# Products for the next chunk's maxima at other steps of the two spare PSUM banks

## The reference

```
q, k, v   = Wq x + bq, Wk x + bk, Wv x + bv          # layer 0: 32, 32, 256 channels
attn      = softmax(q^T k, over the query index i)    # scores[b, i, j], axis=1
x1        = gamma * (v attn) + x

theta     = conv1x1(x1)                               # layer 1: 32 channels, 4096 positions
phi, g    = maxpool2(conv1x1(x1))                     # 32 and 128 channels, 1024 positions
attention = softmax(theta^T phi, over j)
y         = gamma * conv1x1(g attention) + x1
```

## Time and profile before

| | |
|---|---|
| median of 3 runs | 2719.68 us (2712.09 to 2726.18) |
| profiled execution | 2717.54 us, of which the span is 2715.7 us |
| mean granted TensorE clock | 0.986 |
| PE busy | 2610.4 us, 96% |
| DVE busy | 2036.5 us, 75% |
| ACT busy | 1741.6 us, 64% |
| POOL busy | 1979.4 us, 73% |
| products for maxima, 128x512 into aux (L954) | 1097 |
| reductions of these (L740) | 1097, 683 ns each |

### The profile page before, as it was taken

How to read it: one execution, slowest core, us unless ns; L and a number is a source line. 1 busy time by engine, 2 the same in 40 slices (tenths; PEclk the granted TensorE clock), 3 DMA queues, 4 the chain that set the end, 5 groups by cost and what they waited for, 6 DMA issues and landing times.

```text
span 2715.7 us, 38345 instructions
## 1 busy us (share of the span) xinstructions
PE 2610.4 (96%) x11632; PEld 2078.7 (77%) x11632; DVE 2036.5 (75%) x3351; ACT 1741.6 (64%) x3171; POOL 1979.4 (73%) x1546
## 2 busy tenths in 40 slices
PE   7999999989999999998999999999899999999988
PEld 6788788777678888887678888888667888888765
DVE  7678777767777777776777777787677777877665
ACT  5566666667756666666775666666676666666566
POOL 3677777767867777775886777777588777777668
PEclk9999999999999999999999999999899999999989
DMA  2000000012110000001220000000121000000011
GB/s 90 1 16 16 17 24 17 24 40 71 63 32 21 20 23 18 17 16 41 70 78 24 17 24 16 17 16 17 47 79 63 16 16 16 17 17 16 17 47 63
DMA packets 45552, 85.28 MB, mean 31 GB/s; under 512 B 5032, under 2 KB 5160, under 8 KB 45352
## 3 DMA queue, kind: packets, MB, share of 16 engines
q1 hardware_dynamic: 37720, 68.41, 7.6%
q10 hardware_dynamic: 7632, 14.42, 1.8%
HBM read 49.03 MB, written 33.55 MB: 30 GB/s over the span
## 4 chain that ended last, share of the span: by engine, by line
PE 78%; DVE 12%; issue 5%; ACT 2%; POOL 1%; DMA 1%; SPq 0%; ACTq 0%; POOLq 0%; DVEq 0%
PE o_ps L914 16%; PE o_ps L917 16%; PE o_ps L918 16%; PE s_ps L891 9%; PE aux L954 8%; DVE mx L740 5%; DVE acc L702 3%; PE aux L928 2%; PE aux L992 1%; PE aux L975 1%; PE aux L932 1%; DVE aux L781 1%; PE aux L971 1%; POOL prob_l L502 1%; ACT queries L589 1%
## 5 line engine op out<-in xcount | busy, mean ns | idle before, releaser
L502 POOL TENSOR_TENSOR prob_l<-prob,prob_h 128x512 fp32r<-128x512 f32 x1280 | 1665.7, 1309 | 628.5 <-ACT prob_h L564 622.2
L561 ACT ACTIVATE prob<-s_ps 128x512 f32<-128x512 f32 x1280 | 766.8, 599 | 781.9 <-PE s_ps L891 779.8
L740 DVE TENSOR_REDUCE mx<-aux 128x1 f32<-128x512 f32 x1097 | 749.0, 683 | 290.9 <-PE aux L954 285.6
L914 PE MATMUL o_ps<-prob_h,vh 128*128 128x512 f32 x2304 | 912.4, 396 | 0.7
L917 PE MATMUL o_ps<-prob_l,vh 128*128 128x512 f32 x2304 | 903.6, 392 | 2.5 <-POOL prob_l L502 2.2
L918 PE MATMUL o_ps<-prob_h,vl 128*128 128x512 f32 x2304 | 900.8, 391 | 0.0
L702 DVE TENSOR_TENSOR acc<-prob,acc 128x512 f32<-128x512 f32 x1152 | 790.1, 686 | 61.9 <-ACT prob L561 49.6
L564 ACT ACTIVATE prob_h<-s_ps 128x512 fp32r<-128x512 f32 x1280 | 764.4, 597 | 0.0
L891 PE MATMUL s_ps<-queries,keys 128*128 128x512 f32 x1280 | 514.8, 403 | 22.9 <-DMA queries<-nm_turned 11.6
L914 PEld LDWEIGHTS o_ps<-prob_h,vh 128*128 128x128 f32 x2304 | 434.7, 189 | 101.2 <-ACT osb L575 9.8
L917 PEld LDWEIGHTS o_ps<-prob_l,vh 128*128 128x128 f32 x2304 | 434.4, 189 | 101.1 <-POOL prob_l L502 11.6
(11 more groups left out here) (131 smaller groups left out, 1845.4 us busy)
## 6 DMA issues: line engine op xcount, KB each, us to landing
xa<-x SPq DMA_DIRECT2D x32, 512.0 KB, 3.7
spill<-xa SPq DMA_DIRECT2D x32, 512.0 KB, 2.7
xa<-spill SPq DMA_DIRECT2D x32, 512.0 KB, 3.7
y<-xa SPq DMA_DIRECT2D x32, 512.0 KB, 2.8
xp<-x ACTq DMA_DIRECT2D x26, 512.0 KB, 3.7
queries<-nm_turned SPq DMA_DIRECT2D x236, 1.0 KB
xp<-x SPq DMA_DIRECT2D x2, 512.0 KB, 9.5
prob<-w_in ACTq DMA_DIRECT2D x1, 640.0 KB, 5.9
```

Source lines behind the costliest of these rows:

```text
L502: nc.gpsimd.tensor_tensor(out=prob_l[:, i, :], in0=prob[:, i, :], in1=prob_h[:, i, :].bitcast(f32), op=ALU.subtract).then_inc(pl_ready, 1)
L561: nc.scalar.activation(prob[:, i, :], s_ps[s][:, :], ACT.Exp).then_inc(p_ready, 1)
L740: ins = nc.vector.tensor_reduce(out=dst, in_=bank[:, :], axis=AX.X, op=ALU.max)
L914: mm(o_ps[ct][:, :], value(vh, l, t, ct), prob_h[:, i, :], start=t == 0, stop=False)
```

## The change

Layer 0, chunks n = 0 to 6 (28 of them): the X0 products of steps 3 and 6 are taken out. One X0 product is added at step 25, place 3, which is now the last of the 32. One X1 product is added at step 18 (step 17 where n is 0), place 1. The number of products is 32 as before, their order over keys and queries is kept.

```diff
             if n + 1 < NCH:
-                steps = sorted(([(t, 3 if t else 1, X0) for t in range(25)]
-                         + [(t, 1, X1) for t in (8, 11, 14, 22, 23, 24, 25)]), key=lambda e: e[:2])
+                steps = sorted([(t, 3 if t else 1, X0) for t in range(26) if t not in (3, 6)]
+                               + [(t, 1, X1) for t in (8, 11, 14, 18 if n else 17, 22, 23, 24, 25)], key=lambda e: e[:2])
                 for i, (t, place, at) in enumerate(steps):
                     put(g + t, place, maxima(0, b, n + 1, i // SUBS, i % SUBS, at))
                 put(g + 27, 1, Job("M", 0, b, n + 1, 0))
```

## The result

The changed kernel takes 2755.59 us in the median (4 runs, 2751.05 to 2761.41), the kernel before 2721.3 us (4 runs). The ratio is 1.0131 with a 95% interval of 1.0096 to 1.0166: 1.3% slower, where 2753 us and 1.2% were forecast. The profiled execution of the changed kernel has a span of 2759.5 us, 43.8 above that of before.

The account below looks back on a forecast made before the run. TensorE, busy for 96% of the span, was taken as the bound, with its waits on VectorE deciding. -15.9 + 29.8 + 17.4 + 1.8 = +33.1 us on 2717.5 gives 2750.6, plus 2.1 for the median: 2753 us, range 2734 to 2766.

Parts of the forecast that it names:

- step 6: Chunks n = 1 to 6: the product's wait on VectorE's reduction goes, 0.66 us a chunk, 15.9 us won.
- step 18: Chunks n = 1 to 6: the moved X1 product waits on K1L, then G1 on its reduction; 29.8 us lost.
- step 29: Maxima arrive later, so the next chunk's first score waits 0.62 us longer for DMAs; 28 chunks, 17.4 us lost.
- the chunks n = 0 of images 1 to 3: The product at step 17 shares X1 with the V0 behind it: 0.6 us a chunk, 1.8 us lost.
- Term 2: Two new waits in step 18, 0.79 us behind K1L and 0.44 ahead of G1; 24 chunks, 29.8 us lost.
- Term 1: The wait of step 6 goes with the products of steps 3 and 6 taken out; 24 chunks, 15.9 us won.
- A: Rival: step 18 is free, as K1L ends 0.75 us earlier; 2723 us, no change; chance 0.06.
- B: Rival: the maxima arrive in time, with 0.6 us of slack in the way of the DMAs; 2735 us; chance 0.06.
- C: Rival: the costs at step 18 and step 29 are both hidden; 2706 us, faster; chance 0.03.
- D: Rival: the granted clock falls at the new stops of step 18, 41 us more, 2794 us; chance 0.03.

Follow-up runs that it names:

- place_2: The changed kernel with the X1 product of step 18 at place 2 instead of 1: 2752.85 us, 1.0093 of the kernel before.
- no_17: The changed kernel with the X0 product of step 17 moved to X1 at step 9 in chunks n = 1 to 6: 2746.7 us, 1.0103 of before.
- only_6_out: The kernel before with only the X0 product of step 6 moved to X1 at step 9, chunks n = 1 to 6: 2704.71 us, ratio 0.9947.
- last_at_25: The kernel before with only the X1 product of step 11 moved to X0 at step 25, place 3, chunks n = 0 to 6: 2737.7 us, ratio 1.0054.
- gain_alone: The kernel before with the X0 products of steps 3 and 6 moved to X1 at steps 9 and 12, chunks n = 1 to 6: 2703.33 us, ratio 0.9915.
- all_chunks: Against before, X0 products of steps 3 and 6 moved in chunks n = 1 to 7, last product X0's at step 24: 2694.27 us, ratio 0.9905.

## Why the prediction was right

**The terms.** Per chunk n = 1 to 6, forecast and measured from start to start in the changed kernel: step 6, -0.66 and -0.70; step 18, +1.24 and +1.20; step 29, +0.62 and +0.65. In the chunks n = 0 of images 1 to 3 beyond step 29, +0.6 and +0.43 (3.24 us in three chunks less three times 0.65). Times their counts, 24, 24, 28 and 3: -16.8 + 28.9 + 18.1 + 1.3 = +31.5, where +33.1 was forecast. The step 6 term was 0.04 short, since the small gap of 0.03 in step 5 went as well. In the chunks n = 0 the loss stands at step 17, as forecast (0.41 us a chunk by its starts); the 0.2 us that the prediction allowed there for the release by the low part did not come. The prediction also said that no product of step 6 would wait on a reduction; that holds in the chunks that it changes, and the four chunks n = 7 still have the wait. The three places hold when each is edited alone.

**Term 2 was right in its sum and told as two prices that are one.** The prediction worked out 0.79 behind K1L and 0.44 ahead of G1, both right to 0.03 us in the trace. That reads as if each could be saved by itself. place_2 shows that the first can't, and no_17 that the second can, but that half of what it frees is paid back at the first. The bound is VectorE's queue through the step.

**Term 1 named both removals.** only_6_out shows that step 6's alone brings 15.4 of the 16.8 us.

**The rivals.** A (K1L earlier because VectorE has less to do) fell at the row that the prediction named: in the changed kernel the reduction ahead of K1L (three operations ahead by the rows, not two) again starts after 0.52 us of idle waiting for TensorE. B (slack in the maxima's way) fell with last_at_25, and C with both. D, that the granted clock falls at the stops of step 18: this row of the changed kernel, busy time by stretch, is the whole chunk with its stops, at a granted clock of 1.00:

```profile
877.00:941.00 64.00, 62.85 (x274) 50.52 (x274) 49.44 (x80) 39.84 (x75) 46.56 (x37) 1.00 0.05 18
```

Stops that cost 0.66 us at step 18 and 0.64 us at step 29, between dense matmuls, leave the clock at its upper level, 2.4 GHz, here and in all 24 chunks n = 1 to 6. What the Trainium skill says of the clock (TensorE: Matmul & The Clock Gate, Part 1), that it is given for activity and taken away when idle, is not contradicted; at stops of this length nothing was taken away.

**The other rule.** VectorE's addition at 914.21 and the reduction behind it at 914.82 are 0.61 us apart at 0.70 recorded, so in the changed kernel too the next operation starts before the recorded end of the one ahead. The Trainium skill's "The DRAIN you can't avoid" (VectorE: DVE Perf Modes), read strictly, would have G1 start 0.09 us later than it does; the trace disagrees with that reading, but not with the passage as a whole, which says that an operation that is not held starts earlier. Nor do all pairs overlap: the two operations behind K1L start only after the recorded end of the one ahead, at 913.49 and 914.21 (0.78 and 0.72 us apart), and so do the two behind it in no_17, at 908.19 and 908.91. So 0.60 us is not the pace of every pair. Why these two are slower was not tested.

**What stays open.** The 11.5 us that layer 1 took longer in the one trace are put down to the run, because runs of one and the same kernel scatter by 19 us along their mean clock. That the change has no effect at all on layer 1, as by the moment at which its short phases fall, was not tested by an edit of its own. The traces speak against it: over all ten layer 1 takes 506.3 to 519.7 us in no order of the edits, 507.2 in no_17, which holds the change but for one product, and 517.0 in gain_alone, which has none of its costs.

## What to carry to other kernels

Where a bank is shared, cost a moved product by three moments: when its last reader ends, when its own reader can start in that engine's queue, and when the next writer wants the bank. Ask of each wait what else would hold the same instruction if it went: an engine's queue that bounds a whole stretch hands a wait from one end to the other. And before the last of a set of results is moved, follow it to its consumer, through the small operations and the DMAs; a way that shows no wait may still have no slack, and a true wait elsewhere on the same way gives its length.

## What was not expected of the hardware

In some of the traces a short operation of VectorE in layer 1 of the last image is recorded several times longer than its usual 0.7 us. These rows are VectorE and TensorE in gain_alone:

```profile
2622.19 6.28 DVE L698 TENSOR_TENSOR acc<-prob 128x512 f32<-128x512 f32 x1
```

```profile
2628.70 1.62 PE L971 MATMUL aux<-ident,rsum 128*128 128x128 f32 x6 [4.78 <-DVE rsum L775]
```

It is the first addition of a chunk (L698), which has a mean of 0.99 us over the whole trace of before; here TensorE stops for 4.78 us behind it. Among the ten traces of this case there are eight such additions, of 4.8 to 6.3 us, all of that line and all in the last image. Layer 1 of that image took 99.5 to 99.9 us in the four traces that have none, 105 us in the four that have one, and 110 us in the two that have two. They follow no edit: the traces with none are those of before, last_at_25, no_17 and all_chunks. What holds the addition the runs do not show. Each costs about 5 us. They are probably part of why two runs of one kernel differ by more than the smaller of these edits; with one trace of each kernel that is not shown.
